# A DLRM tower: thirteen held tables for ten, one buffer of gathered rows for two, and gathers that start at the end of a turn's second gram

## The reference

```python
e = stack([tbl_f[ids[:, f]] for f in range(26)], axis=1)
combined = concatenate([dense[:, None, :], e], axis=1)        # 2048 x 27 x 128
z = einsum('bfd,bgd->bfg', combined, combined)[:, iu, ju]     # the 351 pairs f < g
h = concatenate([z, dense], axis=1)                           # 479 wide
h = maximum(h @ W_top1 + b_top1, 0)                           # 512
h = maximum(h @ W_top2 + b_top2, 0)                           # 256
y = h @ W_top3                                                # 1
```

## Time and profile before

| | |
|---|---|
| median of 3 runs | 527.81 us (524.25 to 528.95) |
| the profiled execution | 531.68 us, of which the span of instructions is 529.9 us |
| busy, of the span | PE 365.6 us (69%), POOL 253.9 (48%), DVE 242.4 (46%), ACT 153.4 (29%) |
| mean granted TensorE clock | 0.826 of full speed |
| DMA | 33.3 MB, 16.8 of them gathered in 256 indirect DMAs |

### The profile page before, as it was taken

The page is one execution under the profiler, slowest core; times in us unless marked ns, Lnnn a source line. Parts: engine busy times, 40 slices in busy tenths (PEclk is TensorE's granted clock), DMA queues, the critical chain, the costliest instruction groups (busy, mean ns, idle before and its releaser), DMA issues.

```text
span 529.9 us, 13987 instructions
## 1 busy us (share of the span) xinstructions
PE 365.6 (69%) x6224; PEld 335.2 (63%) x6224; DVE 242.4 (46%) x172; ACT 153.4 (29%) x269; POOL 253.9 (48%) x260
## 2 busy tenths in 40 slices
PE   6774232298826988288936987299737987399937
PEld 5663122298824988188925977199626976299826
DVE  4994015084431837065542927076332927084220
ACT  2542101122412224122513324133322333133522
POOL 6887747326463465525563556526462656400000
PEclk9997556588976989689876989599775989699978
DMA  7971113121131211212130212212131212100000
GB/s 209 274 232 47 51 33 101 31 54 48 36 92 26 69 45 49 75 35 70 33 96 25 74 45 59 70 29 69 33 90 28 76 40 74 55 15 0 15 15 1
DMA packets 23322, 33.32 MB, mean 63 GB/s; under 512 B 6565, under 2 KB 15397, under 8 KB 23303
## 3 DMA queue, kind: packets, MB, share of 16 engines
q0 software_dynamic: 8192, 16.79, 11.8%
q1 hardware_dynamic: 14926, 16.20, 11.1%
q10 hardware_dynamic: 186, 0.09, 0.1%
HBM read 29.97 MB, written 0.01 MB: 57 GB/s over the span
## 4 chain that ended last, share of the span: by engine, by line
PE 53%; issue 20%; another core or an unknown queue 13%; DVE 7%; ACT 6%; SPq 1%; DMA 1%; ACTq 0%; DVEq 0%
PE psum L455 29%; PE psum L480 11%; DVE onehot L274 4%; PE psum L469 3%; PE psum L545 2%; PE psum L493 2%; ACT feats L333 2%; PE psum L494 2%; PE psum L495 2%; DVE hot_lo L261 2%; PE psum L537 1%; ACT gram L333 1%; ACT h L375 1%; ACT dense_hi L333 1%
## 5 line engine op out<-in xcount | busy, mean ns | idle before, releaser
L249 POOL DMA_INDIRECT rows<-table,idx x256 | 253.7, 991 | 207.4 <-PE psum L469 106.1
L274 DVE TENSOR_TENSOR onehot<-ids_b,psum 125x2048 fp32r<-125x2048 int16 x80 | 179.8, 2281 | 12.7 <-PE psum L455 6.8
L257 DVE COPY gram<-psum 26x416 f32<-26x416 f32 x64 | 37.4, 585 | 205.4 <-PE psum L480 203.9
L333 ACT ACTIVATE feats<-psum 128x512 f32<-128x512 f32 (+1 forms) x120 | 77.5, 690 | 162.7 <-PE psum L455 98.1
L480 PE MATMUL psum<-feats 128*26 128x26 f32 x4096 | 65.5, 208 | 72.0 <-issue 67.9
L455 PE MATMUL psum<-onehot,hot_hi 125*128 125x256 f32 x640 | 101.9, 303 | 14.0 <-issue 9.4
L480 PEld LDWEIGHTS psum<-feats 128*26 128x26 f32 x4096 | 55.3, 121 | 84.8 <-issue 78.4
L455 PE MATMUL psum<-onehot,hot_lo 125*128 125x256 f32 x640 | 96.9, 294 | 3.9 <-issue 3.8
L455 PEld LDWEIGHTS psum<-onehot,hot_hi 125*128 125x128 f32 x640 | 88.5, 204 | 16.1 <-issue 10.7
L455 PEld LDWEIGHTS psum<-onehot,hot_lo 125*128 125x128 f32 x640 | 87.6, 200 | 8.3 <-issue 7.3
L333 ACT ACTIVATE gram<-psum 26x416 f32<-26x416 f32 (+1 forms) x72 | 35.5, 494 | 80.5 <-PE psum L480 57.7
(11 more groups left out here) (26 smaller groups left out, 168.2 us busy)
## 6 DMA issues: line engine op xcount, KB each, us to landing
lows<-table SPq DMA_DIRECT2D x10, 448.0 KB
rows<-table,idx POOLq DMA_INDIRECT x256
ids_b<-hot_ids SPq DMA_DIRECT2D x8, 384.0 KB
ids_b<-hot_ids SPq DMA_DIRECT2D x8, 256.0 KB
rows<-dense SPq DMA_DIRECT2D x16, 64.0 KB
lows<-w SPq DMA_DIRECT2D x1, 1024.0 KB
pairs<-gram SPq DMA_DIRECT2D x16, 39.0 KB
lows<-table SPq DMA_DIRECT2D x10, 52.0 KB
```

What stands on the lines that cost most here:

```text
L249: pool.indirect_dma_start(out=rows[t][:, f, :], out_offset=None, in_=tables[f - 1], in_offset=bass.IndirectOffsetOnAxis(ap=idx[:, 2 * s + ...
L257: return nc.vector.tensor_copy(o, x)
L274: nc.vector.tensor_tensor(onehot[f % SLOTS][0:HP_ROWS, :, :], ids_b[0:HP_ROWS, f:f + 1, :].to_broadcast([HP_ROWS, HC, SB]), psum[0:HP_ROWS ...
L333: return nc.scalar.activation(o, x, ACT.Copy)
```

## The change

- The number of held tables goes from 10 to 13, all that have 1000 rows. A unit of held tables is still two, so there are seven, the last with one. The gathered tables are 13, in four groups with the dense feature (4, 4, 4 and 2).
- There is one buffer `rows`. Tile 1's gathers wait until tile 0's group has been transposed, and the other way round.
- POOL waits ahead of a turn's gathers until the second gram of the turn before has finished (`gram_done[1]`). They are then the gathers of the same turn, not of the next.
- Layer 3 comes behind the second gram; two groups of tile 1 stand ahead of the dense step, the last ahead of layer 2.
- There are 3 one-hot buffers. The compare ahead of the copies of the second gram is gone; it moves to the next turn's first.
- `pairs_lo` lies on `pairs` itself. So SP's moves of the first gram wait until layer 1b of the turn before has read it (`mlp_b`), not only for the split.
- SP loads tile 1's dense feature at the start of its turn. The 32 transposes ahead of turn 0 are gone.

```diff
-NUM_HOT = 10
+NUM_HOT = 13
...
-    WARM = 32
-    SLOTS = 4
+    SLOTS = 3
+    AHEAD = 4
...
-    TILE0 = [("hot", 0), ("rows", 0, 0), ("hot", 1), ("rows", 0, 1), ("hot", 2), ("rows", 0, 2), ("hot", 3),
-             ("rows", 0, 3), ("hot", 4), ("rows", 0, 4)]
+    TILE0 = [("hot", 0), ("hot", 1), ("rows", 0, 0), ("hot", 2), ("rows", 0, 1), ("rows", 0, 2), ("hot", 3),
+             ("rows", 0, 3), ("hot", 4), ("hot", 5), ("hot", 6)]
...
-             + [("layer", "1b")] + TILE1[1:2] + [("dense",)] + TILE1[2:3] + [("layer", "2")] + TILE1[3:]
-             + [("layer", "3"), ("gram", 1)])
+             + [("layer", "1b")] + TILE1[1:3] + [("dense",)] + TILE1[3:] + [("layer", "2"), ("gram", 1), ("layer", "3")])
...
-        rows = [sb(f"rows{t}", [P, NR, D]) for t in range(2)]
+        rows = sb("rows", [P, NR, D])
...
+        pairs_lo = pairs[:, :, :].bitcast(fp32r)
-        pairs_lo = sb("pairs_lo", [P, ZC, SB], fp32r)
...
+        def wait_rows_free(eng, s, t, g):
+            if t == 1:
+                wait_rows(eng, s, 0, g)
+            elif s > 0:
+                wait_rows(eng, s - 1, 1, g)
...
-                elif s > 0:
-                    sp.wait_ge(pairs_split, s)
+                elif t == 0:
+                    sp.wait_ge(mlp_b, 2 * s - 1)
...
             for s in range(TURNS):
+                load_dense(s, 1)
                 if s + 1 < TURNS:
                     load_ids(s + 1, 0)
-                    load_dense(s + 1, 0)
...
                     load_ids(s + 1, 1)
-                    load_dense(s + 1, 1)
+                    load_dense(s + 1, 0)
...
                 for t in range(2):
+                    if s > 0 and t == 0:
+                        pool.wait_ge(gram_done[1], 2 * s)
                     for g, features in enumerate(GROUPS):
-                        if s > 0:
-                            wait_rows(pool, s - 1, t, g)
+                        wait_rows_free(pool, s, t, g)
...
                 rest_of_dense(s)
-                if not last:
-                    compare(s + 1, 3, False)
                 copy_gram(dve, copy, 1, s, 1, first)
...
-            for n in range(WARM):
-                nc.tensor.transpose(psum[:, HP[0], 0:P], ident_sb[:, :], ident_sb[:, :])
```

More of the change, by code:

```diff
@@ L43, in dlrm_tower @@
     HOT = [list(range(f, min(f + 2, NH))) for f in range(0, NH, 2)]
-    assert NG == 5 and len(HOT) == 5 and C1 == 4 and C2 == 2
-    TILE0 = [("hot", 0), ("rows", 0, 0), ("hot", 1), ("rows", 0, 1), ("hot", 2), ("rows", 0, 2), ("hot", 3),
-             ("rows", 0, 3), ("hot", 4), ("rows", 0, 4)]
+    assert NG == 4 and len(HOT) == 7 and C1 == 4 and C2 == 2
+    TILE0 = [("hot", 0), ("hot", 1), ("rows", 0, 0), ("hot", 2), ("rows", 0, 1), ("rows", 0, 2), ("hot", 3),
+             ("rows", 0, 3), ("hot", 4), ("hot", 5), ("hot", 6)]
     TILE1 = [("rows", 1, g) for g in range(NG)]
@@ L185, in load_dense @@
             def load_dense(s, t):
-                if s > 0:
-                    wait_rows(sp, s - 1, t, 0)
-                sp.dma_start(rows[t][:, 0, :], dense[2 * s + t, :, :]).then_inc(dense_in[t], 16)
+                wait_rows_free(sp, s, t, 0)
+                sp.dma_start(rows[:, 0, :], dense[2 * s + t, :, :]).then_inc(dense_in[t], 16)
             def wait_gram(s, t):
@@ L212, in _ @@
             load_ids(0, 1)
-            load_table(4)
-            load_dense(0, 1)
-            for f in range(5, NH):
+            for f in range(4, NH):
                 load_table(f)
@@ L249, in _ @@
                                 pool.indirect_dma_start(
-                                    out=rows[t][:, f, :], out_offset=None, in_=tables[f - 1],
+                                    out=rows[:, f, :], out_offset=None, in_=tables[f - 1],
                                     in_offset=bass.IndirectOffsetOnAxis(ap=idx[:, 2 * s + t, f - 1:f], axis=0),
@@ L406, in turn @@
                         if first:
-                            for f in (2 * n[0] + SLOTS, 2 * n[0] + SLOTS + 1):
+                            for f in (2 * n[0] + AHEAD, 2 * n[0] + AHEAD + 1):
                                 if f < NH:
@@ L424, in _ @@
             copy(psum[0:HP_ROWS, ROWS_P, 0:HC], hot_rows_sb[0:HP_ROWS, :]).then_inc(row_numbers, 1)
-            for f in range(SLOTS):
+            for f in range(AHEAD):
                 round_hot(f)
@@ L468, in transposes @@
                 for m, f in enumerate(GROUPS[g]):
-                    mm = nc.tensor.transpose(psum[:, bank, m * P:(m + 1) * P], rows[t][:, f, :], ident_sb[:, :])
+                    mm = nc.tensor.transpose(psum[:, bank, m * P:(m + 1) * P], rows[:, f, :], ident_sb[:, :])
                 mm.then_inc(rows_done, 1)
             def grams(s, t, first):
-                wait_feats(pe, s, "rows", t, NG - 1)
+                wait_feats(pe, s, *(TILE0, TILE1)[t][-1])
                 for h in range(2):
```

## The result

The changed kernel takes 551.15 us (median of 4 runs, 550.36 to 552.38) against 527.42 for the kernel before (4 runs beside it): ratio 1.045 [1.042, 1.048], slower. I had forecast 513 us. The profiled execution took 552.38 us, span 550.6, mean granted clock 0.857 of full speed (before: 531.68, 529.9, 0.826).

A forecast was written before the change was run, and what follows sets the result against it. Bursts of POOL's gathers were taken to hold up PE's completions. Turn 0 63.3 + seven turns of 59.7 + tail 27.2 + first pass 3.0 = 511.4, with 1.8 outside 513 us; 8-in-10 range 456 to 548.

The forecast's parts named there:

- That gathers, and nothing else, made turn 4 longer than turn 7: Kernel before: turn 4's extra 19.7 us over the last turn come from gathers holding PE's completions, not from busy engines.
- About 3 us into a burst PE's completions come to a near stop: During unbroken POOL gathers, PE's completions nearly stop after about 3 us and come back when POOL pauses.
- At 4.0 per us to T + 38: Held phase beside gathers: PE does 4.0 instructions per us, not 8.4, until 38 us after T, the second gram's end.
- Release at 38: Held phase: the second gather burst ends at T + 36.3 and PE is released 1.7 us later; T ends the second gram.
- three tables at 1.9 end at T + 43.6: End of held phase: the last three tables run at 1.9 us each, done 43.6 us after the second gram's end.
- Turn 0 ends at 63.3: Turn 0: without gathers for turn 1, both grams run free and it ends at 63.3 us in place of 106.5.
- Free turn 43.8: A changed turn with no gathers holding it takes 43.8 us, reckoned from turn 7's 39.1 plus three more tables.
- Tail 27.2: Behind the last turn: 25.5 us plus a 1.7 us wait of the second gram's copies for pair moves, 27.2 us.
- First pass 3.0: Turn 1 of the kernel before was 4.9 us longer than turn 4; 3 us of that were kept.
- Last turn 20.6 us longer: The last turn, 39.1 us before without gathers beside it, becomes like the others: a loss of 20.6 us.
- the third: Rival: the long burst holds PE beyond its end, both releases 1.8 us later; turn 65.6, total 554 us; chance 0.15.
- The first: Rival: held tables hardly mind gathers; turn 51.9, total 458 us, chance 0.20; with no cost at all 410, chance 0.05.

The follow-up runs named there:

- b_none: The kernel before with its gathers in the first turn alone, later turns transposing the first turn's rows: 371.94 us, ratio 0.704 to the kernel before.
- best1: The changed kernel with two small fills behind each gather (pitch 1.59 us) and some row transposes set later: 489.17 us, ratio 0.920 to the kernel before.
- a_none: The changed kernel with POOL's gathers in turn 0 alone, later turns transposing what turn 0 left: 413.25 us, ratio 0.784 to the kernel before.
- a_plain_pool: The changed kernel with each indirect DMA replaced by a plain one of the table's first 128 rows, still from POOL: 416.76 us, ratio 0.791.
- best3: As best1, but a turn's 20th gather waits until the first gram is done: 455.78 us, ratio 1.175 to the kernel before on its chip.

## Why the prediction was wrong

- *That gathers, and nothing else, made turn 4 longer than turn 7:* right, b_none.
- *"About 3 us into a burst PE's completions come to a near stop":* wrong as a mechanism. I read it from ACT's late copies alone. PE's own rows show full speed for 8 us beside held tables and then one matmul in about 1.4 us: 65 matmuls free in the first burst, then 6 in the 8 us to 284.28. Beside a gram it comes sooner, after 53 records in 0.6 us in best1.
- *"At 4.0 per us to T + 38":* this term came out right, by luck. From T + 3.4 to T + 38 (T = 267.66) I had 159 matmuls of held tables and transposes, and turn 4 has 159. The first stretch had fewer than I reckoned (62 to T + 22, not 74), the stretch between the bursts fewer too (31, not 40), the second burst more (66, not 45).
- *"Release at 38", "three tables at 1.9 end at T + 43.6":* this step failed. I let PE be back at full speed 1.7 us behind each burst. Tile 1's first gather went out at T + 20.0, not T + 16.6, and the second release came at T + 40.0. The 38 matmuls then left took 8.7 us, at a granted clock of 0.50 until 315.3, with 0.8 us of waiting for a compare, where I had 5.6 us for the last three tables; layer 1a began at T + 48.5. Those 4.9 us are all but 0.4 of what the turn lacks. The lower clock behind a stall was no term of mine. A turn is 65.0 us on average (7 turns, 455.0 us), not 59.7: 34 of the 38 us.
- *Turn 0 ends at 63.3:* 69.5; 6 us. No gram was held by gathers, but each had a gap of 2 us put down to issue near its end, beside a block on the instruction queue, and ACT waited 8.1 us for the pairs. That the gaps would be gone was wrong: they are there without gathers too (12.0 us in b_none, all in turns 0 and 1).
- *Free turn 43.8:* 44.3 in a_none. *Tail 27.2:* 25.6. *First pass 3.0:* 3.9. Sum: 69.5 + 455.0 + 25.6 = 550.1.
- *Last turn 20.6 us longer:* 25.5. It gave back more than half of what turn 0 gained (37 us).
- *Three compares* are what I said turn 4 has and turn 7 has not; there are four (10 against 6). Nothing in the sum hangs on it.
- *Rivals:* the third (554 us) came out nearest, for its reason in part: near standstill, and releases at 3.1 and 2.2 us. The first had in its favour that held tables went well beside 22 gathers in turn 0; but there DVE set the pace, and PE took few instructions in a microsecond.
- *The Trainium skill, "SBUF — State Buffer", section "SBUF: two separate sides":* I took turns 4 and 7 to disagree with it. The runs agree with the page: a_plain_pool moves the same bytes on the same queue and takes 416.8 us, where a_none takes 413.3, so the data's way into SBUF was not what slowed PE. The Trainium skill's page "DMA: Bandwidth & Descriptors", section "SWDGE vs HWDGE vs iDMA", says that for DMAs from GpSimd, plain ones too, software on GpSimd builds the descriptors; no run here shows why building those of an indirect one should keep instructions from PE, and that stays open.

What the change was after did happen: the grams were freed, from 67.9 to 7.9 us. But the time went into the held phase, because a burst of 13 stalls PE for some 10 us where the short ones of before there (3, 8 and 5) did so little, and 41 us of table work bought 18 us less of stall.

## What to carry to other kernels

Beside indirect DMAs from GpSimd, ask how many instructions TensorE must get in each stretch, and look in its own timeline for gaps of "issue"; moving an unbroken run of gathers only moves the stall. A pause of 0.64 us behind each gather, or bursts of no more than four with pauses as long between, cost hardly more than the mildest dose beside matmuls of 256 columns; beside small matmuls (the grams) the same pause was not enough. Price a burst by letting one kernel try another dose in each turn, and time the kernel before and after on the same chip: best3 at 455.8 us looks 14% faster than the 527 of another chip, and is 17% slower than before on its own.

## What the runs showed that I had not expected

- The hold is not the same everywhere: the kernel before took 527 to 531 us on three chips and 388.6 on a fourth, where b_none's 372 (another chip) is nearly reached. The fourth was used once, so whether it is the chip or something in its condition then stays open, and the changed kernel was not run there.
- Pacing repairs the held phase all at once: from a pitch of 1.33 us to one of 1.59 the turn falls by 9 us, and slower pitches gain nothing more.
- Held matmuls of 128 columns, back to back for 13 tables a turn, left the granted clock at 0.50 (480.5 to 572.0 us: PE busy for 90.7 of 91.5); the same work in matmuls of 256 columns runs at 1.00. The split kernel took 973.8 us, its unsplit twin 460.4.
